# Router logits as extra columns of two projections, and routing in batches of twelve and four tiles

## The reference, cut to what matters

```python
x = x + memory(adaln_attention(x, cond))     # 16 heads of 64, one key and value head, relative bias
x = x + ffn(moe(x, cond))                    # 8 experts, top 2 of a softmax, plus a shared MLP

# memory(x): retrieval with a decayed, strictly causal product, per sequence
retrieved = einsum(scores * weights, x @ Wv.T); return retrieved @ Wo.T * out_scale
# moe(x, g): routing
logits = (x @ wt.T + repeat(g @ wg.T)) / 2
topk_w, topk_idx = top_k(softmax(logits), 2)
# each token: weighted sum of leaky(x @ gate) * (x @ up) @ down of its two experts, plus the shared MLP
# ffn(h) = relu(h @ W1 + b1) @ W2 + b2
```

## Time and profile before

| | us |
|---|---|
| median of 3 runs | 550.3 (549.51 to 552.85) |
| the profiled execution's own time | 548.08 |
| its span, first to last instruction | 546.2 |

### The profile page before, as it was taken

How to read it: one execution, slowest core, us unless ns; L and a number is a source line. 1 busy time by engine, 2 the same in 40 slices (tenths; PEclk the granted TensorE clock), 3 DMA queues, 4 the chain that set the end, 5 groups by cost and what they waited for, 6 DMA issues and landing times.

```text
span 546.2 us, 10833 instructions
## 1 busy us (share of the span) xinstructions
PE 481.4 (88%) x3449; PEld 428.7 (78%) x3449; DVE 377.9 (69%) x943; ACT 249.2 (46%) x510; POOL 276.7 (51%) x265
## 2 busy tenths in 40 slices
PE   4866889999999999999998838579999669999997
PEld 2755779988989899988888727479989549898986
DVE  5786999899999999998866327467766434444522
ACT  3325575654555564654551311346665324444442
POOL 3747878787978878787811735700000434334100
PEclk9977999999999999999988977889999969999999
DMA  8460006436190811000000311255673212212111
GB/s 271 96 164 6 25 2 213 144 121 235 28 327 0 293 62 29 0 29 2 31 1 5 118 63 67 86 185 174 192 226 114 90 40 67 68 50 86 30 40 38
DMA packets 51613, 52.14 MB, mean 95 GB/s; under 512 B 6644, under 2 KB 49014, under 8 KB 51576
## 3 DMA queue, kind: packets, MB, share of 16 engines
q1 hardware_dynamic: 47956, 42.98, 24.8%
q0 software_dynamic: 3072, 8.39, 4.8%
q10 hardware_dynamic: 548, 0.28, 0.2%
HBM read 22.03 MB, written 29.62 MB: 95 GB/s over the span
## 4 chain that ended last, share of the span: by engine, by line
PE 37%; issue 19%; POOL 16%; DVE 12%; another core or an unknown queue 4%; ACT 3%; DMA 2%; POOLq 1%; SPq 1%; DVEq 0%; ACTq 0%
PE bank L302 6%; PE bank L303 6%; PE bank L304 6%; POOL biasm L512 5%; PE bank L307 4%; POOL rn L551 4%; PE bank L308 3%; PE bank L1636 3%; PE bank L1365 2%; POOL wu_l L516 2%; POOL pr L537 2%; POOL yg L573 1%; DMA slot_y<-yb 1%; POOL rs L555 1%
## 5 line engine op out<-in xcount | busy, mean ns | idle before, releaser
L573 POOL DMA_INDIRECT yg<-slot_y,yrow x32 | 34.3, 1071 | 120.1 <-DMA slot_y<-yb 75.5
L551 POOL TENSOR_TENSOR rn<-sc,half 128x5 f32<-128x5 f32 (+1 forms) x32 | 55.3, 1729 | 27.7 <-DVE sc L1011 27.7
L1248 DVE TENSOR_TENSOR hl<-hw,hh 128x512 fp32r<-128x512 f32 x32 | 22.2, 693 | 57.3 <-ACT hw L810 54.3
L808 ACT ACTIVATE hh<-bank,late 128x512 fp32r<-128x512 f32 x32 | 22.0, 688 | 53.8 <-PE bank L1636 40.3
L302 PE MATMUL bank<-wqkv_h,xnT_h 128*128 128x384 f32 x96 | 39.2, 408 | 4.6 <-DVE sim L988 4.6
L564 POOL DMA_INDIRECT slot_x<-xs,posi x32 | 31.7, 990 | 21.2 <-DVE posi L1110 12.0
L546 POOL TENSOR_TENSOR sim<-sim,mx 128x1040 f32<-128x1040 f32 x16 | 31.3, 1956 | 19.4 <-DVE mx L995 19.0
L671 ACT ACTIVATE sq<-bank 128x384 f32<-128x384 f32 (+1 forms) x48 | 22.7, 474 | 40.1 <-PE bank L304 25.0
L512 POOL TENSOR_TENSOR biasm<-bias,mneg 128x1040 f32<-128x1040 f32 x16 | 35.6, 2222 | 1.8 <-issue 1.8
L307 PE MATMUL bank<-wout_h,oT_h 128*128 128x256 f32 x128 | 33.9, 300 | 2.4 <-DVE oT_l L1026 2.4
L1365 PE MATMUL bank<-kblk,qT 128*64 128x130 f32 x512 | 32.9, 282 | 3.2 <-POOL kblk L530 2.1
(11 more groups left out here) (311 smaller groups left out, 1591.7 us busy)
## 6 DMA issues: line engine op xcount, KB each, us to landing
slot_x<-zrow SPq DMA_DIRECT2D x4, 4352.0 KB, 14.5
xq<-slot_x SPq DMA_DIRECT2D x40, 128.0 KB, 2.1
slot_y<-yb SPq DMA_DIRECT2D x20, 256.0 KB, 2.4
fstage<-in_f_W SPq DMA_DIRECT2D x4, 512.0 KB, 4.0
out<-p_all SPq DMA_DIRECT2D x8, 256.0 KB, 2.1
xs<-in_x SPq DMA_DIRECT2D x1, 1536.0 KB, 9.5
raw_out<-in_c_Wout SPq DMA_DIRECT2D x1, 1024.0 KB, 8.7
stage<-in_m_wgate SPq DMA_DIRECT2D x8, 128.0 KB
```

Of the source, the lines that this page charges most:

```text
L551: e.tensor_tensor(rn[:, lo:hi], sc[:, lo:hi], half[:, lo:hi], ALU.pow).then_inc(sems['rn'], 1)
L573: e.indirect_dma_start(out=yg[:, g % 2, r, t, :], out_offset=None, in_=ydram.ap()[:, :], in_offset=bass.IndirectOffsetOnAxis(ap=yrow[:, g ...
```

## The change

The router's logits are no longer a product of their own. They are a sum of three parts, each made where its factor is multiplied anyway:
- from x: the attention projection gets E = 8 more columns, the router weights (`wqkv_h`, `wqkv_l` grow to QKV + E, bank 3). They see the normalized x, so mean and scale of each token (`ln1`, copied to `stats`) undo the normalization later, in `token_logits`. ScalarE copies `stats` and the eight columns (`xlog`) in each step.
- from the retrieval: the folded weights `wvo` get E columns, Wv Wo wt; the addition to `xs`, now D + E wide, carries them.
- from the condition: `cond_logits`, computed in steps 0 and 1, is put into the extra columns of `xs` beforehand.

Gone are `logits(g)`, `wt_hl` and the split of the router weights. The batches are twelve and four tiles. Batch 0's sums stand in step 15 on VectorE (`before_sums`), its top at the end of step 15 (`before_norms`), its ranks and places in step 16. GpSimd issues four scatters behind step 16 and the rest behind the pipeline. `edge_units` lets both halves of the splits of units 8 and 9 run in steps 16 and 17. Batch 1 is routed right behind the pipeline. `x_transpose`, `x_upper` and `x_lower` of the first three groups move, and the `late` load moves up.

```diff
-BATCHES = ((0, 8), (8, 8))
+BATCHES = ((0, 12), (12, 4))
+FIRST_SCATTERS = 2
-        xs = sb('xs', [P, NT, D])
+        xs = sb('xs', [P, NT, D + E])
...
+        def edge_units(i):
+            if i < 0 or i > NT + 1:
+                return (None, None)
+            if i >= NT:
+                return (i - NT // 2, i - NT // 2)
+            return (i // 2, None) if i % 2 == 0 else (None, i // 2)
...  GpSimd
+            def first_scatters():
+                e.wait_ge(sems['st_zero'], 16 * ZPARTS)
+                e.wait_ge(sems['pos'], 1)
+                scatter(0, FIRST_SCATTERS)
-                if part is not None and part[1] == 1:
-                    split_unit(part[0])
+                if part[1] is not None:
+                    split_unit(part[1])
-            e.wait_ge(sems['st_zero'], 16 * ZPARTS)
-            for b, (t0, n) in enumerate(BATCHES):
-                e.wait_ge(sems['pos'], due(b + 1))
-                ...
-            split_unit(U - 1)
+            pipeline(e, body, {..., NT: first_scatters})
+            scatter(FIRST_SCATTERS, BATCHES[0][1] - FIRST_SCATTERS)
+            e.wait_ge(sems['pos'], 2)
+            scatter(*BATCHES[1])
...  ScalarE
+            after_exp = {NT - 1: lambda: router_exp(0)}
+            def cond_rows():
                 e.wait_ge(sems['ld_late'], 16 * 2)
+                e.wait_ge(sems['lg_t'], 1)
+                e.activation(cg[:, :, :], bank[7][0:2, 0:NT * E].rearrange('p (t e) -> p t e', e=E), ACT.Copy).then_inc(sems['cg'], 1)
                 if live(1):
+                    e.wait_ge(sems['ln1_rs'], due(i + 2))
+                    e.activation(at_tile(stats, i + 1), ln1[:, :], ACT.Copy)
                     e.wait_ge(sems['xnT'], due(i + 2))
...
+                    e.activation(at_tile(xlog, i + 1), bank[NB3][:, QB:QB + E], ACT.Copy)
                     for b, r in ((0, 0), (0, 1), (1, 0), (1, 1)):
-            pipeline(e, body, {-1: wout_upper, 0: decay_exp, 1: decay_log, 2: lambda: [decay_power(), wt_upper()], NT - 1: first_x, NT: lambda: router_exp(0), NT + 1: lambda: x_upper(2)})
+            pipeline(e, body, {-1: wout_upper, 0: lambda: [decay_exp(), cond_rows()], 1: decay_log, 2: decay_power, NT - 1: lambda: x_upper(0), NT + 1: lambda: x_upper(1), LAST_I: lambda: x_upper(2)})
+            router_exp(1)
             unit_gate(0)
...  VectorE
-            before_sums = {-1: before_first_sums, 0: wvo_lower, 1: decay_sum, 2: decay_rate, 3: wt_lower, NT: lambda: x_lower(1), NT + 1: lambda: router_places(0)}
-            before_lower = {LAST_I: lambda: x_lower(2)}
-            before_norms = {-1: fold_qk}
+            before_sums = {-1: before_first_sums, 0: wvo_lower, 1: decay_sum, 2: decay_rate, NT - 1: lambda: [token_logits(), router_logits(0)], NT: lambda: router_places(0)}
+            before_norms = {-1: fold_qk, NT - 1: lambda: router_top(0)}
-                    e.tensor_tensor(at_tile(xs, i - 3), bank[4][:, 0:D], at_tile(xs, i - 3), ALU.add).then_inc(sems['x1'], 1)
+                    e.tensor_tensor(at_tile(xs, i - 3), bank[4][:, 0:D + E], at_tile(xs, i - 3), ALU.add).then_inc(sems['x1'], 1)
+            def token_logits():
+                rlink(e.tensor_tensor(tsum[:, :], stats[:, :, 2], stats[:, :, 3], ALU.mult))
+                rlink(e.tensor_tensor(xlog[:, :, :], xlog[:, :, :], over_experts(tsum[:, :], NT), ALU.mult))
+                rlink(e.tensor_tensor(score[:, :, :], wsum[:, :].rearrange('p (o e) -> p o e', o=1).to_broadcast([P, NT, E]), stats[:, :, 0:1].to_broadcast([P, NT, E]), ALU.mult))
+                rlink(e.tensor_tensor(xlog[:, :, :], xlog[:, :, :], score[:, :, :], ALU.add))
-                rlink(e.reduce_sum(lg[:, ts, :], logits_of(b), AX_X))
+                rlink(e.tensor_tensor(lg[:, ts, :], xlog[:, ts, :], xs[:, ts, D:D + E], ALU.add))
-            pipeline(e, body, {-2: after_first_stats, NT - 1: lambda: x_lower(0), NT: after_values})
+            pipeline(e, body, {-2: after_first_stats, NT: lambda: x_lower(0), NT + 1: lambda: x_lower(1)})
+            router_logits(1)
+            x_lower(2)
+            router_top(1)
             unit_leak(0)
+            router_places(1)
+            unit_product(0)
             x_lower(3)
...  TensorE
+            def cond_logits():
+                e.wait_ge(sems['p_const'], 1)
+                e.wait_ge(sems['cg'], 1)
+                e.matmul(bank[7][:, NT * E:2 * NT * E], pair_of[:, :], cg[:, :, :].rearrange('p t e -> p (t e)'), start=True, stop=True)
+                for k in range(KD):
+                    last = e.matmul(bank[7][:, 2 * NT * E:2 * NT * E + E], ones[:, :].bitcast(F32), wt_raw[:, k, :], start=k == 0, stop=k == KD - 1)
-            while_retrieving = {NT: lambda: x_transpose(1), NT + 1: third_x, LAST_I: first_gate}
-            before_values = {NT - 1: first_x, NT: lambda: logits(0)}
+            while_retrieving = {NT + 1: lambda: x_transpose(1), LAST_I: third_x}
+            before_values = {1: cond_taken, NT - 1: first_x, NT: lambda: ranks(0)}
             e.wait_ge(sems['x1'], due(NT))
+            up(0)
+            gate(1)
             x_transpose(3)
-            logits(2)
-            up(0)
-            logits(3)
-            gate(1)
             up(1)
+            ranks(1)
             gate(2)
             up(2)
-            ranks(1)
             down(0)
```

More of the change, by code:

```diff
@@ L1300, in after_first_projection @@
                 e.wait_ge(sems['ld_att'], 16 * 5)
+                e.wait_ge(sems['ld_cols'], 16 * 2)
+                for k in range(KD):
+                    for j in range(KD):
+                        e.matmul(bank[4][:, k * E:(k + 1) * E], raw_att[:, 3, j, k * P:(k + 1) * P], wt_raw[:, j, :], start=j == 0, stop=j == KD - 1)
                 for k in range(KD):
@@ L1313, in after_first_projection @@
                         last = e.matmul(bank[6][:, i * D:(i + 1) * D], raw_att[:, 2, k, i * P:(i + 1) * P], woT[:, k, :], start=k == 0, stop=k == KD - 1)
+                e.wait_ge(sems['v_fold'], 1 + KD)
+                for i in range(KD):
+                    for k in range(KD):
+                        last = e.matmul(bank[7][:, i * E:(i + 1) * E], raw_att[:, 2, k, i * P:(i + 1) * P], wowt[:, k, :], start=k == 0, stop=k == KD - 1)
                 last.then_inc(sems['t_fold'], 1)
```

187 lines of the change are left out of this document (86 added, 101 removed).

## The result

The changed kernel took 559.8 us (median of 4 runs, 557.2 to 561.9) against 550.8 (4 runs, 549.5 to 552.9) beside it: ratio 1.016, 95% interval 1.010 to 1.021. It is 1.6% slower. Beside the kernel before in another session it took 562.2 (4 runs, 560.1 to 563.1; 1.021, 1.015 to 1.026). The profiled execution took 561.91 us with a span of 560.2, so 14.0 more span than before.

The account below looks back on a forecast made before the run. TensorE was taken to bound the attention loop, its late signals during scatters the early-unit stage. Last x1 at 310.6, 36 us of units and 7.5 of late signals gave slot start 354 (-8), span 538, execution 540, median 542.3; range 534 to 556.

Parts of the forecast that it names:

- Start: Ahead of the loop: added small matmuls, scalings and a copy, less removed router-weight work, cost net +0.6 us, bounds 0 to +1.5.
- Each step: Attention loop: eight more columns on TensorE cost +0.5 us in all, bounds 0.2 to 1.3; ScalarE's two copies have cover.
- Step 15: VectorE's logits sums (+0.2), router_top(0) (5.2) and x_lower(0) (1.3) put step 16's statistics near 281.7, not 277.57.
- Step 17: GpSimd: unit 8's split ends near 293, four scatters (5.2) follow, then the power for rs2 near 298.5 instead of 296.61.
- Step 18: x_lower(1) (1.3 us) ahead of VectorE's decay product, x_transpose(2) (1.0) and gate(0) ahead of TensorE's value projection; last x1 at 309.5.
- Scatters: Behind unit 9's split, 28 scatters 1.3 us apart, the last starting at 341; first slot copy at 347 at the earliest.
- Units: Early dense units, last x1 to first slot copy: 36 us without late signals, from 56.6, reaching 346.6.
- Late signals: Early-unit stage: TensorE's signals arriving late during scatters cost 7.5 us, between none and 15 or more; slot start 354.
- The two rules weighed: Trainium skill: increments serialize at some 26 ns each; GpSimd descriptors locked out by VectorE's two-port operations, taken as nothing, otherwise 5.6 us.
- one long hold: Early units: signals held to the burst's end at 343, slot start 368, median 556 to 559; chance 0.16.
- the wash: Rival for the early units: late signals cost all 15 us, slot start 361.6 against 361.9, median 550; chance 0.24.
- The slots and the feed-forward stay: The stretch from the first slot copy to the end: taken as unchanged.

Follow-up runs that it names:

- e2: The changed kernel with the start's additions (weight products, conditioning rows and their spreading) moved behind step 0's scores: 561.6 us, ratio 1.024 to the kernel before.
- e1: The changed kernel with no scatters inside the steps; step 16's four go behind the last step: 558.9 us, ratio 1.022 to the kernel before.
- f1: e1 with the scatters in groups, each behind the first waiting for something VectorE computes from TensorE's results: 553.4 us, ratio 1.006 to the kernel before.
- f2: e1 with at most two scatters in flight: 548.3 us, ratio 0.996 to the kernel before.
- e3: The changed kernel with plain transfers to fixed rows instead of indexed scatters (output not the reference's): 536.7 us, ratio 0.978 to the kernel before.
- f3: The kernel before with plain transfers to fixed rows instead of indexed scatters (output not the reference's): 542.0 us, ratio 0.983 to the kernel before.
- h3: g1 with a wait for all landings ahead of every sixth scatter in place of two in flight: 541.3 us, ratio 1.006 to the kernel before.
- g1: The changed kernel with the start moved as in e2, three plus three scatters early, at most two in flight: 547.3 us, ratio 0.995 to the kernel before.
- g2: The kernel before with at most two scatters in flight: 544.7 us, ratio 0.988 to the kernel before.
- h2: The kernel before with a wait for all landings ahead of every sixth scatter: 546.3 us, ratio 1.011 to the kernel before.
- h1: e1 with a wait for all landings ahead of every sixth scatter: 550.3 us, ratio 1.022 to the kernel before.
- h4: h3 with the wait for all landings ahead of every fourth scatter instead: 544.2 us, ratio 1.011 to the kernel before.
- f4: f1 with the start moved as in e2, two scatters ahead of unit 8's split and two behind step 17's root: 545.0 us, ratio 0.988.
- i1: h3 with drained groups of nine scatters instead of six: 541.6 us, ratio 0.983 to the kernel before.
- g3: e1 with at most four scatters in flight: 563.6 us, ratio 1.023 to the kernel before.
- g4: e1 with a one-column memset on GpSimd ahead of each scatter: 561.4 us, ratio 1.019 to the kernel before.

## Why the prediction was wrong

It forecast 542.3 and a first slot copy at 354; the copy came at 372.94 and the time was 559.8. Of the 18.9 us, 7.4 lie ahead of the last x1 (its end at 318.01 and not 310.6) and 11.5 in the late signals behind it. By its steps:

- **Start** (+0.6, bounds 0 to 1.5): failed, 4.2 in the profile, 3.8 as a mean. Step 1's matmuls, taken as 0.6, hold TensorE for 1.67, and the stall there is some 2.6. The eight products of eight columns ahead of the first fold (1.71 us), and eight more behind it, had no price at all. e2, which moves all of them behind step 0's scores, gets 2.8 of the 3.8 back, so that much was their place and not their work.
- **Each step** (+0.5 in all, bounds 0.2 to 1.3): the mechanism right, the size too high; nothing was added. `den` from step 1 to the step at 230 takes 170.08 us, before 170.26; the ScalarE copies are covered.
- **Step 15** (step 16's statistics at 281.7): they came at 287.07. Of the 5.4 us, 4.2 are the start's, which the 281.7 left out. Most of the rest is router_top(0), taken as 5.2 from eight tiles; it takes 6.2 with twelve, its multiply 1.35 us while GpSimd multiplies `pr`.
- **Step 16** (TensorE makes good the 4.1 by which VectorE is late): right. The statistics came 9.5 us later than before, the output projection behind the step 5.2 (295.55, before 290.31), so 4.3 were made good.
- **Step 17** (root at 298.5): the mechanism was right, the size was not. Unit 8's split was to end near 293 and ends at 298.89, because ScalarE's half comes at 296.11; again 4.2 are the start's. The root at 304.12 costs the last x1 4.5 us (e1) to 7.3 (f1 and f2, 75.7 us from `den`). These have one order up to there; what differs is TensorE's granted clock in the last stretch, 0.54 in e1 (306.0 to 310.8, nearly all at the 1.2 GHz level) and 1.00 in f1 (305.0 to 307.4, at 2.4 GHz).
- **Step 18** (+1.3 and +1.0): the mechanism right, both sizes low. x_lower(1) kept the decay product until 311.87, 1.7 us behind the end of its matmul (310.18), and x_transpose(2) took 1.91 us at a granted clock of 0.50.
- **Steps 15 to 18 together** (+4.3): +8.6.
- **Scatters** (306 to 342, unbroken): 312 to 336, and 342 to 351. Unit 9's split ended at 312.03, and the premise that batch 1's places are ready in time failed with the signal of ranks(1).
- **Units** (36 us without late signals): right in number, 36.4 in e3 and 36.0 from the end of the last x1. In part that is luck. It took 13.3 us for late signals out of the stage before, where f3 shows 8.5; so the order without logits and with the split elsewhere, taken as 7.3, must be worth 12.1 (48.5 - 36.4).
- **Late signals** (7.5 us): this is the step that decided. The stage takes 55.4 us, so they cost 19.0. I priced an average delay by what stood under each burst, halved. What the experiments show goes by how long the burst has run: signals on time for the first 7.2 us, late from 7.3 to 10.6 us on, then one at a time in order, the last of them 1.6 to 5.1 us behind the end. In after the signal of ranks(1), on which everything waited, stood behind those of two transposes and came at 340.62.
- **The two rules weighed.** `rk` was held 15.2 us behind one increment, and the recorded signals of e3 and h3 come within 20 ns of their instructions' ends; the rule of the Trainium skill ("TensorE: Matmul & The Clock Gate", The cost: per-tile semaphore tail) does not describe this wait. The rule of the Trainium skill on GpSimd's descriptors ("SBUF — State Buffer", Who interferes with whom) cost next to nothing here: scatters beside VectorE's work took 0.06 us more in all in after, where the prediction's case for it had 5.6. But it is not nothing. In all profiles together, the first scatter of each burst left out, 40 of 498 took 0.04 to 0.39 us more than the usual 0.96; when each of these began, VectorE was in an operation that reads two tiles of SBUF (mostly `hl`), and none of the 421 that began without one was longer.
- **The rival "one long hold"** named the right mechanism, its place and 556 to 559 us, with a chance of 0.16. Its condition was wrong: ranks(1) did not get through before the hold, and that did not fall back to the wash. It made two bursts of one, the second without a wait on a held signal, behind a last x1 that was 7.4 us later than taken. Nor was it one hold until the end: two signals came through at 327.2 and 334.9. The first slot copy at 372.9 is past the 368 of the rival.
- **"The slots and the feed-forward stay"**: they took 3.0 us more. The granted clock of TensorE is what differs, 0.50 in the slots' first stretch (the 1.2 GHz level) where the kernel before had 1.00 (2.4 GHz):

```profile
376.00:380.00 4.00, 4.00 (x20) 4.00 (x20) 1.53 (x3) 0.98 (x2) 0.00 (x0) 0.50 0.31 92
```

```profile
365.00:369.00 4.00, 4.00 (x37) 4.00 (x35) 2.79 (x7) 2.24 (x5) 0.00 (x0) 1.00 0.82 296
```

In both, TensorE does nothing but the slots' matmuls for these 4 us, 20 in after and 37 in before. Ahead of them it had waited 1.96 and 1.18 us for ScalarE and VectorE in after, 1.33 and 1.28 in before, so these waits do not tell the two apart; in e1 the first products came without the slow stretch. It is not the change's: three of the twenty profiles keep 1.00 behind the first slot copy (before, e1 and g1, 184.3, 183.6 and 185.7 us from it to the end), the other seventeen show 0.50 there (186.1 to 188.3 us), three with the old order among them (f3, g2, h2). What granted it is open.

## What to carry to other kernels

Before moving work in front of a long burst of indexed scatters, look in the trace for readers that start long after their TensorE instruction ended, and ask how far into the burst the signal falls. Break such a burst into groups of at most some 7 us, each ended by a wait for its own landings: in this kernel that cost 1.7 to 2.2 us a gap and removed a wait of 15. Since signals that are held come in order, the one on which most depends should stand early in a group; no run here tried that by itself. And do not add an engine's late work to a queue that serves the critical step (the scatters ahead of the root), nor small products into the first steps: count every instruction that a step is put in front of.

## What the runs showed of the hardware

- TensorE's signals are held while GpSimd issues indexed scatters (128 rows of 1 KB, 1.27 us apart) without a gap. Instructions of TensorE itself go on: in after it issues transposes, an up projection, ranks(1) and a gate between 321 and 329, while their readers stand. Plain transfers of the same bytes from the same queue hold nothing (e3, f3, in stretches of up to 10.7 us), nor do indexed ones in drained groups of four or six (h1 to h4). The first signal late by over 1 us is that of an instruction ending 7.3 (f1, f4), 8.0 (before), 8.2 (i1), 9.4 (after) or 10.5 to 10.6 us (g3, e1) into an unbroken stretch; the latest that was still on time ended 10.1 us into one (g3). Whether the time or the number of scatters counts was not told apart, nor what the path of the signal shares with them; the trace names no releaser.
- Held signals come in the order of their instructions, some of them while the burst goes on: in g4, with 32 scatters from 303.74 to 344.40, at 315.26, 324.50, 329.45 and, 1.2 us behind the end, 345.61. Once a burst has ended, those still held come close together: in before four of them from 323.47 to 323.70, 0.08 us apart, in i1 four from 318.85 to 321.11, 0.7 to 0.8 us apart.
- A hold can cost more than the wait that shows it (19.0 us of stage for 15.06 in after), because it also decides when the next scatters can be issued. An earlier start does not help: e1 had the last x1 6.7 us earlier and its first slot copy 0.3.
- The kernel before, unchanged, had medians of 550 to 551 us in all sessions but one, on at least three chips, and 537.8 in that one, on another. A ratio is only good beside runs of the same session.
